# Banded attention unrolled, with its maxima by 32 queries times 160 keys and both score products issued alternately

## The reference, cut to what matters

```
qkv = x @ Wqkv + bqkv;  q, k, v = split(qkv, 3);  16 heads of 8
scores = einsum("bhid,bhjd->bhij", q, k) * 8 ** -0.5
scores = where(|i - j| <= 64, scores, most negative number)
attn = softmax(scores);  out = einsum("bhij,bhjd->bhid", attn, v)
return out @ Wout + bout
```

## Time and profile before

| | |
|---|---|
| median of 3 runs | 861.48 us (861.15 to 864.0) |
| the profiled execution's own time | 861.29 us |
| its span, first to last instruction | 859.5 us |
| attention, first instruction to the next part's first DMA | 0 to 291.88 us |
| busy over the span | PE 77%, DVE 61%, POOL 42%, ACT 40% |
| mean granted TensorE clock | 0.904 of 2.4 GHz |

### The profile page before, as it was taken

One profiled execution on the slowest core, in us unless ns is written; L12 is line 12 of the kernel. 1 busy time (PEld: TensorE's weight loads), 2 busy tenths in 40 slices (PEclk: granted clock), 3 DMA queues, 4 the chain that ended last, 5 costly groups with the idle time before them and its releaser, 6 DMA issues. The chain is left out here.

```text
span 859.5 us, 18332 instructions
## 1 busy us (share of the span) xinstructions
PE 660.1 (77%) x7554; PEld 384.0 (45%) x7554; DVE 525.7 (61%) x1094; ACT 344.9 (40%) x522; POOL 359.2 (42%) x330
## 2 busy tenths in 40 slices
PE   0617888888888279976977498058998988999995
PEld 0302444444445179876876234023333344444442
DVE  8647667676664733342413667869999974406266
ACT  1421433444344573242414552346544536434320
POOL 9202444444444300000001253228999974966530
PEclk9967999999999559997977689669999999999998
DMA  3156552000000364000000640000000000000000
GB/s 76 37 107 108 89 72 32 0 0 0 0 0 2 111 199 100 3 4 2 4 4 5 261 112 0 0 1 0 0 1 0 0 1 1 1 0 1 12 13 25
DMA packets 17327, 29.76 MB, mean 35 GB/s; under 512 B 3248, under 2 KB 13168, under 8 KB 16240
## 3 DMA queue, kind: packets, MB, share of 16 engines
q1 hardware_dynamic: 17264, 28.87, 14.1%
HBM read 24.54 MB, written 4.19 MB: 33 GB/s over the span
## 5 line engine op out<-in xcount | busy, mean ns | idle before, releaser
L474 ACT ACTIVATE pr_exp<-at_psum 128x1024 f32<-128x1024 f32 x68 | 69.6, 1023 | 131.9 <-PE at_psum L559 131.9
L366 DVE TENSOR_REDUCE pr_neg_max<-at_psum 128x4 f32<-128x1024 f32 x68 | 83.2, 1225 | 49.8 <-PE at_psum L541 49.8
L316 POOL TENSOR_SCALAR_AFFINE_SELECT pr_exp<-pr_exp 128x512 f32<-128x512 f32 x68 | 47.1, 692 | 159.0 <-ACT pr_exp L474 159.0
L1493 POOL TENSOR_TENSOR all_phi_b<-all_phi_b,mo_work 128x512 f32<-128x512 f32 x56 | 71.1, 1269 | 43.3 <-ACT mo_work L1699 38.6
L749 POOL TENSOR_TENSOR all_x<-all_x,ff_x_blocks 128x512 f32<-128x512 f32 x3 | 3.8, 1263 | 173.0 <-ACT ff_x_blocks L940 173.0
L1514 PE MATMUL all_psum<-all_phi,mo_xt 128*128 128x512 f32 x128 | 67.1, 651 | 7.3 <-ACT mo_work L1681 5.6
L536 PE MATMUL at_psum<-band_mask,all_ident_bf 128*128 128x512 bf16 x136 | 43.1, 400 | 38.3 <-DVE pr_q_window L359 38.3
L1463 POOL TENSOR_TENSOR mo_work<-mo_work,mo_max 128x1024 f32<-128x1024 f32 x32 | 61.3, 1916 | 22.1 <-DVE mo_max L1755 22.1
L1547 PE MATMUL all_psum<-mo_xt,all_phi_centred 128*128 128x512 f32 x128 | 65.4, 591 | 0.0
L1600 PE MATMUL all_psum<-mo_work,mo_y_slots 128*128 128x512 f32 x128 | 62.5, 595 | 1.8 <-DVE mo_work L1803 1.8
L1699 ACT ACTIVATE mo_work<-all_psum 128x512 f32<-128x512 f32 x64 | 37.7, 601 | 60.6 <-PE all_psum L1547 60.6
(11 more groups left out here) (339 smaller groups left out, 1340.2 us busy)
## 6 DMA issues: line engine op xcount, KB each, us to landing
all_expert_w<-in_expert_w SPq DMA_DIRECT2D x1, 4096.0 KB, 18.3
ff_b_up<-in_b_up SPq DMA_DIRECT2D x1, 2048.0 KB, 10.2
ff_a_up<-in_a_up SPq DMA_DIRECT2D x1, 2048.0 KB, 16.1
ff_w_down<-in_w_down SPq DMA_DIRECT2D x2, 1024.0 KB, 20.5
at_q_stack<-parts_scratch SPq DMA_DIRECT2D x24, 64.0 KB
at_k_stack<-parts_scratch SPq DMA_DIRECT2D x24, 64.0 KB
at_q_stack<-parts_scratch SPq DMA_DIRECT2D x12, 128.0 KB
at_k_stack<-parts_scratch SPq DMA_DIRECT2D x12, 128.0 KB
```

The lines of the kernel that those rows point to most:

```text
L316: nc.gpsimd.affine_select(out=e[:, g, :, 0, :], in_=e[:, g, :, 0, :], compare_op=ALU.is_ge, fill=0.0, base=0, pattern=[[0, GH], [-1, P]], ...
L366: nc.vector.tensor_reduce(negm[:, GH * g:GH * g + GH].rearrange("p (u r) -> p r u", r=2), psum[:, SN + 2 * (g % 2):SN + 2 * (g % 2) + 2, : ...
L474: nc.scalar.activation(e[:, g, :, :, :].rearrange("p h j q -> p (h j q)"), psum[:, ST:ST + 2, :].rearrange("p b n -> p (b n)"), ACT.Exp).t ...
L1493: nc.gpsimd.tensor_tensor(tot[:, ch % 2, :], first, ec[:, ch % 2, j, :], ALU.add).then_inc(added, 1)
```

## The change: what it does

- **Loop.** All 17 windows (`NW`) are written out on every engine, in 8 units of two heads instead of 4 groups of four. The copies of keys, queries and values to fixed places go, with the tiles for them. Before the first step, the naturals of windows 0 and 1 are computed; step s then computes those of window s + 2.
- **Natural product.** Each unit has 8 products of 32 queries and 160 keys (64*32, 49 rows used) in place of four products of 256 keys per four heads. The mask is no longer written by TensorE; VectorE adds it in one `tensor_tensor_reduce` per head that also takes the maximum.
- **Transposed product.** The maxima's three parts are three more rows of the stacks, so the selector products go, and so does their selector. A unit is four products of 52 rows and 128 columns (64*128), with three PSUM banks in rotation for them and three for the naturals.
- **Order on TensorE.** `scores` issues one transposed product, two natural ones, one transposed one and so on; the natural ones belong to the heads of the other row half (`other`).
- **Maxima.** `take_maxima` on ScalarE copies the transposed maxima and issues two DMAs on ScalarE's queue that put them into the query stack.
- **Projections.** x comes in three DMAs. The parts go straight from SBUF to the stacks, high parts first; the HBM scratch is gone. Only the edges of the stacks are filled by GpSimd; six DMAs write the flag row and the rows of ones. The bias of v is folded into a bias row, and the scale into the exponential. W_qkv and its bias are laid out on the host so that the rows come in the right order.
- **Output.** `project` runs one tile at a time inside the loop, and 12 of the 16 tiles are normalised before the last window is done.
- **Warm-up.** 16 products of 512 columns (`keep_warm`) stand before the first naturals and again before step 0.

The diff, cut to its core:

```diff
-    scratch = nc.dram_tensor("parts_scratch", [3, 2, P, T], BF16).ap()
-    kw = b.sb("k_window", [P, 2, NP, 2 * P], BF16)
-    qw = b.sb("q_window", [P, 2, NP, P], BF16)
...
-        with eng.Fori(0, (NS - 3) // 2) as i:
-                nc.vector.tensor_copy(kw[:, wp, :, :], ks[:, :, bass.ds(w * P, 2 * P)])
-                nc.vector.tensor_copy(qw[:, wp, :, :], qs[:, :, bass.ds(w * P, P)]).then_inc(win, 1)
...
+    NW = NT + 1
+    NU = 8
+    QC, WIN = 32, 160
+    FLAG, PARTS = 48, 49
+    WARM = 16
...
+misc_bf = psum[0:3 * H, MISC, 0:64].bitcast(BF16)
+head = lambda m, i: (m % 2, 2 * (m // 2) + i)
+other = lambda m: m ^ 1
...
+def slot_free(pe, n):
+
+    if n < 3:
+        return
+    if n - 3 in proj_at:
+        pe.wait_ge(y_ready, proj_at[n - 3] + 1)
+    else:
+        pe.wait_ge(sn_free, n - 2 - sum(k <= n - 3 for k in proj_at))
...
+        sp.dma_start(x[:, 0:4, :], rows[:, 0:4, :]).then_inc(x_loaded[0], 16)
...
+        for half in range(2):
+            p0 = 64 * half
+            sp.dma_start(ks[p0 + FLAG:p0 + FLAG + 1, :, :], flags[:, :].unsqueeze(1).broadcast_to([1, NP, (NT + 2) * P])).then_inc(rows_in, 16)
+            sp.dma_start(ks[p0 + PARTS:p0 + PARTS + 3, :, :], ones[:, :].unsqueeze(1).broadcast_to([3, NP, (NT + 2) * P])).then_inc(rows_in, 16)
+            sp.dma_start(qs[p0 + FLAG:p0 + FLAG + 1, :, :], ones[0:1, 0:NW * P].unsqueeze(1).broadcast_to([1, NP, NW * P])).then_inc(rows_in, 16)
...
+        def stack(group, kind):
+            r0, r1 = STACKS[group]
+            sp.wait_ge({"h": hi_ready, "m": mid_ready, "l": low_ready}[kind], 2 * r1 // 512)
+            for which, (dst, terms, pad) in enumerate(((qs, TERMS_Q, 64), (ks, TERMS_K, P))):
+                for n, k in enumerate(terms):
+                    if k == kind:
+                        for half in range(2):
+                            p0 = 64 * half + DH * n
+                            sp.dma_start(dst[p0:p0 + DH, :, pad + r0:pad + r1], part[k][64 * half:64 * half + 64, which, r0:r1]).then_inc(stacked[group], 16)
...
+        def split(ch):
+            r0, r1 = CHUNKS[ch]
+            n = r1 - r0
+            for w in range(2):
+                src = psum[:, (2, 4)[w] + ch % 2, 0:n]
+                dve.wait_ge(hi_ready, 2 * ch + w + 1)
+                if ch >= 2:
+                    dve.wait_ge(low_ready, 2 * ch + w - 3)
+                v.scalar_tensor_tensor(out=rest[:, ch % 2, w, 0:n], in0=src, scalar=bqk[:, w:w + 1], in1=part["h"][:, w, r0:r1],
+                                       op0=ALU.add, op1=ALU.subtract).then_inc(rest_ready, 1)
+            for w in range(2):
+                dve.wait_ge(mid_ready, 2 * ch + w + 1)
+                v.tensor_tensor(part["l"][:, w, r0:r1], rest[:, ch % 2, w, 0:n], part["m"][:, w, r0:r1], ALU.subtract).then_inc(low_ready, 1)
...
+        def maxima(w, m):
+            n = nat_unit(w, m)
+            if m == 0 and w >= 1:
+                dve.wait_ge(mt_done, w)
+            dve.wait_ge(sn_done, n + 1)
+            k = NU * w + m
+            if k >= 3:
+                dve.wait_ge(sn_free, k - 2)
+            for i in range(2):
+                r, j = head(other(m), i)
+                last = v.tensor_tensor_reduce(out=masked[:, 2 * (k % 3) + i, :], in0=psum[:, SN + n % 3, WIN * i:WIN * i + WIN], in1=mask[:, :], scale=-1.0, scalar=3.0e38,
+                                              op0=ALU.add, op1=ALU.min, accum_out=nm[:, r, 0, j:j + 1])
+            last.then_inc(sn_free, 1)
...
+        def exps(w, m):
+            n = NU * w + m
+            act.wait_ge(st_done, n + 1)
+            if w >= 1:
+                act.wait_ge(pv_done, NG * (w - 1) + m // 2 + 1)
+            nc.scalar.activation(e[:, m // 2, 2 * (m % 2):2 * (m % 2) + 2, :, :].rearrange("p h j q -> p (h j q)"), psum[:, ST + n % 3, :], ACT.Exp, scale=scale).then_inc(exp_done, 1)
+
+        def take_maxima(w):
+            act.wait_ge(mt_done, w + 1)
+            if w >= 2:
+                act.wait_ge(nm_in[w % 2], 32 * (w // 2))
+            nc.scalar.copy(m_t[:, w % 2, :], misc_bf).then_inc(mt_ready, 1)
+            act.wait_ge(mt_ready, w + 1)
             for half in range(2):
+                p0 = 64 * half + PARTS
+                act.dma_start(qs[p0:p0 + 3, :, w * P:w * P + P], m_t[24 * half:24 * half + 24, w % 2, :]).then_inc(nm_in[w % 2], 16)
...
+        take_maxima(0)
+        take_maxima(1)
+        for s in range(NW):
+            for m in range(NU):
+                exps(s, m)
+                if m == 1 and s >= 1 and s + 1 < NW:
+                    take_maxima(s + 1)
+                if m == 2 and s >= 1:
+                    take_values(s - 1)
+                if m == 2 and s >= 3:
+                    take_y(s - 3)
+                if m == 6 and s >= 1:
+                    take_attn(s - 1)
+            if s == NW - 2:
+                ln_y.root(act, 0, 12, 0)
+        take_values(NW - 1)
+        take_y(NT - 2)
...
+        def keep_warm(n):
+
+            for _ in range(n):
+                nc.tensor.matmul(psum[:, 5, :].rearrange("p (k n) -> p k n", k=4), c["identb"][:, :], c["identb"][:, :].unsqueeze(1).broadcast_to([P, 4, P]), start=True, stop=True)
...
+        def natural(w, m, i, q):
+            n = nat_unit(w, m)
+            r, j = head(other(m), i)
+            rows = slice(64 * r, 64 * r + PARTS)
+            k0 = w * P + q
+            return nc.tensor.matmul(psum[q:q + QC, SN + n % 3, WIN * i:WIN * i + WIN], qs[rows, j, k0:k0 + QC], ks[rows, j, k0:k0 + WIN], start=True, stop=True)
+
+        def open_transposed(w, m):
+            n = NU * w + m
+            if m == 0:
+                pe.wait_ge(nm_in[w % 2], 32 * (w // 2 + 1))
+            if n >= 3:
+                pe.wait_ge(exp_done, n - 2)
+
+        def transposed(w, m, i, b):
+            n = NU * w + m
+            r, j = head(m, i)
+            rows = slice(64 * r, 64 * r + PARTS + 3)
+            return nc.tensor.matmul(psum[:, ST + n % 3, 256 * i + P * b:256 * i + P * b + P], ks[rows, j, (w + b) * P:(w + b) * P + P], qs[rows, j, w * P:w * P + P], start=True, stop=True)
...
+        def scores(s, m):
+
+            open_transposed(s, m)
+            if s + 2 < NW:
+                open_natural(s + 2, m)
+            for i in range(2):
+                for b in range(2):
+                    t = transposed(s, m, i, b)
+                    if s + 2 < NW:
+                        natural(s + 2, m, i, 2 * b * QC)
+                        n = natural(s + 2, m, i, 2 * b * QC + QC)
+            t.then_inc(st_done, 1)
+            if s + 2 < NW:
+                n.then_inc(sn_done, 1)
+
+        def values(w, g):
+            if g == 0 and w >= 1:
+                pe.wait_ge(o_ready, w)
+            pe.wait_ge(sel_done, NG * w + g + 1)
+            for b in range(2):
                 for k in range(GH):
                     h = GH * g + 2 * (k % 2) + k // 2
+                    last = nc.tensor.matmul(psum[32 * k:32 * k + DH + 1, PV, P * g:P * g + P], v9[:, w + b, h, :], e[:, g, k, b, :], start=(b == 0), stop=(b == 1))
+            last.then_inc(pv_done, 1)
...
+        for w in range(2):
+            for m in range(NU):
+                naturals(w, m)
+            maxima_t(w)
+        keep_warm(WARM)
+        for s in range(NW):
+            for m in range(NU):
+                scores(s, m)
+                if m == 0 and s >= 1:
+                    values(s - 1, 2)
+                if m == 1 and s >= 1 and s + 1 < NW:
+                    maxima_t(s + 1)
+                if m == 1 and s >= 3:
+                    project(s - 3)
+                if m == 2 and s >= 1:
+                    values(s - 1, 3)
+                if m == 4 and s >= 1:
                     values_nat(s - 1)
+                if m == 4:
+                    values(s, 0)
+                if m == 6 and s >= 1:
                     attn_t(s - 1)
+                if m == 6:
+                    values(s, 1)
+        values(NW - 1, 2)
+        values(NW - 1, 3)
+        project(NT - 2)
+        values_nat(NW - 1)
+        attn_t(NW - 1)
+        project(NT - 1)
```

More of the change, by code:

```diff
@@ L174, in attention @@
+        bv = a.sb("bv", [P, 1])
         wout = a.sb("wout", [P, P])
[L175 to L205, removed]
[L206 to L569 removed]
@@ new lines, in attention @@
+        bout = a.sb("bout", [1, P])
+        bias = a.sb("bias_row", [1, P])
+        one = a.sb("one_row", [1, P])
+        xn = a.sb("xn", [P, NT, P])
+        y = xn
+        xt = a.sb("xt", [P, T])
+        rest = a.sb("rest", [P, 2, 2, 512])
+        part = {k: a.sb(f"part_{k}", [P, 2, T], BF16) for k in "hml"}
+        ones = a.sb("ones", [3, (NT + 2) * P], BF16)
+        flags = a.sb("flags", [1, (NT + 2) * P], BF16)
+        mask = a.sb("mask", [P, WIN], BF16)
+        masked = a.sb("masked", [P, 6, WIN], BF16)
@@ new lines, in attention @@
+        nm = a.sb("neg_max", [P, 2, 3, NP])
+        m_t = a.sb("neg_max_t", [3 * H, 2, P], BF16)
+        e = a.sb("exp", [P, NG, GH, 2, P])
+        rec = a.sb("rec", [P, H])
```

(30 more changed lines are left out.)

640 lines of the change are left out of this document (296 added, 344 removed).

## The result

The changed kernel takes **976.8 us** (median of 4 runs, 975.5 to 980.2) against 861.3 beside it: ratio 1.134, interval 1.130 to 1.139. It is slower by 115 us. The forecast was 776, faster, and its range ended at 900. Rival 2 (the change of form is paid, at 1.2 GHz) had said 984. Medians and ratios here are of the executions within 1.5% of a kernel's fastest, which leaves out one of six of e11_64x32_fill and three of six of e12_64x32_fill_late_sp, and the latter's profile is of one of those left out (837.3 us).

The account below looks back on a forecast made before the run. PE was taken to bound the loop before, ScalarE after. Front end 57, loop 138.5 and end 11.5 make 207 us, 85 less than before: 861.3 − 85 = 776 us; own range 752 to 812, 8-in-10 range 752 to 900.

Parts of the forecast that it names:

- Rival 2: In `scores`: each change of form is paid, at 1.2 GHz; 984 us, about 930 with half the time there; chance 0.18.
- the lower end: PE in the loop: alternating products in opposite row halves costs nothing; PE needs at most 8.3 us per step.
- the upper end: PE in the loop: 0.10 us paid at each of a unit's 8 changes of form.
- triple 0.51: In `scores` at 1.2 GHz: one transposed and two natural products with their changes of form take 0.51 us.
- what lies beside the triples: PE's other work per step (values, transposes, `project`) at 1.2 GHz: 6.5 us.
- 15 steps 330: Loop at 1.2 GHz: 15 steps, 22.9 us each, with some stretches at the upper clock level, take 330 us.
- steps 15 and 16 with the end 27: Last two steps, without naturals, at 9 and 6.5 us, and the attention's end at 11.5.
- step 0 at 57: Front end: step 0 starts near 57 us instead of 73, bounds 49 and 67.
- rival 3: Loop and front end: ScalarE or VectorE stalls more, steps of 9.8 us; 808 us, still faster; chance 0.08.
- the 0.48: VectorE in the loop: each `tensor_tensor_reduce` takes 0.48 us, the upper bound.
- the front end of 65: Before the loop: the front end lasts 65 us rather than 57.
- the step of 8.2: Loop: ScalarE sets the step at 7.3 us, plus 0.9 of PE's waits; 15 steps take 123 us.

Follow-up runs that it names:

- e11_64x32_fill: e7_all_64x32 with eight idle products of 512 columns (64*32) ahead of each unit; 816.6 us, ratio 0.951.
- e12_64x32_fill_late_sp: e11_64x32_fill with the maxima's DMAs on SyncE's queue and the transposition of the normalised output one unit later; 823.4 us, ratio 0.958.
- e1: The changed kernel with natural products in the same row half as the transposed one they alternate with; 979.2 us, ratio 1.141.
- e4: The changed kernel with eleven patterns of 24 products of 128 columns ahead of step 0; each change cost 0.10 us; its kernel time means nothing.
- e3_one_form: The changed kernel with natural products of the transposed form (128 queries, 256 keys), two per unit; 843.7 us, ratio 0.981.
- e7_all_64x32: The changed kernel with each transposed product cut into four of the natural form, 24 products per unit instead of 12; 834.5 us, ratio 0.972.
- e6_one_form_fill: e3_one_form with two idle products of 512 columns ahead of each unit, one in each row half; 821.5 us, ratio 0.957.
- e10_fill_late: e6_one_form_fill with the transposition of the normalised output and ScalarE's copy of it one unit later; 808.6 us, ratio 0.940.

## Why the prediction was wrong

- **The step that failed** is in the part on PE: "I take the lower end, by L559, which is this very product in these halves". L559's halves stream side by side because all eight of its products have one form. The doubt beside it, that no row showed a change between opposite halves, was the case. Runs e1 and e4 put the value at the upper end: 0.10 us per change, in opposite halves as in one. Of PE's time that is 64 × 0.105 × 15 = 101 us. The Trainium skill's rule (TensorEngine Tiling (Array Packing), section Key Properties: changing the tiling mode, not just the tile, drains the engine) agrees with all of e4's patterns; it had been given less weight than a row that was about something else.
- **The clock** was rival 2's second half and came too. Its 0.18 was too little, and the range was drawn to leave it out. The forecast had the loop at 2.4 GHz. The changes are not the whole reason for the lower level: without any inside a unit, e3_one_form and e7_all_64x32 were granted 0.61 and 0.53.
- **Rival 2's terms** against the trace: triple 0.51, measured 0.46, since the change costs 0.10 to 0.11 at 1.2 GHz, not 0.12; what lies beside the triples 6.5 per step, measured 21.8 − 32 × 0.46 = 7.1; 15 steps 330, measured 317; steps 15 and 16 with the end 27, measured 34.9, at a clock of 0.60. In all 984, measured 976.8.
- **Front end**: step 0 at 57, measured 54.72. The first variance chain is over at 8.3 instead of 7, ScalarE's last projection copy ends at 35.2 instead of 38, and a unit of the first naturals takes 0.49 instead of 0.6. The stack's DMAs take 0.64 us of SyncE each, not 0.47, which the warming products hid.
- **VectorE**: `tensor_tensor_reduce` was put at 0.30, with ends of 0.19 and 0.48. Two lie 0.25 us apart (39.72 and 39.97 in the timeline; the 0.32 of one overlaps the next). L401, from which the 0.30 came, has one operand in PSUM and not two. Of rival 3 its terms fall, the 0.48 and the front end of 65; its kind, PE waiting for VectorE and ScalarE, could not show while PE was the bound, and came up once it was faster (e3_one_form, e6_one_form_fill).
- **ScalarE**: exponential 0.60 as said; two DMA issues 1.49 instead of 0.9. Neither was on the path.
- **The forecast of 776** is short for the kernel without a change of form, too. That one measured 843.7, 821.5 with its clock and 808.6 with one wait less. So the step of 8.2 (ScalarE's 7.3 and 0.9 of waits) was a second term put too low, which the first one hid. In the last kernel's profiled execution (812.2) the attention ends at 242.3 instead of 207, 35 later: step 0 starts at 60.6 instead of 57 (4); from window 2's maxima to window 16's 14 periods take 139.3 us instead of 115 (24), one of them 15.9 with PE waiting for the maxima's DMAs and twelve about 9.6; 7 lie in step 0 and the last two steps. Of the 9.6, 8 × 0.21 = 1.7 are the idle products themselves.

## What to carry to other kernels

A row shows two matmuls streaming side by side only for the forms that it holds: before interleaving two kinds of product, ask whether they take the same rows and columns of the array, and if not, either give them one form (even with more products, or with columns that are thrown away) or issue them in long runs. Cost an interleaved stream by its changes, 0.10 us each for the forms here, then look at the granted clock. And an operation that is moved to another queue waits there for all that was issued before it, in the first steps too, where the queue was fullest here (13 us in e12_64x32_fill_late_sp).

## What the runs showed of the hardware that was not expected

- A change of form costs 0.10 us at 2.4 GHz and 0.10 to 0.11 at 1.2 (the triple of 0.34 and 0.46 us): in these kernels it did not scale with the clock. Products of one form cost nothing on top, in whichever half or strip.
- Work that does nothing made a kernel faster: with 0.21 us of idle products per unit the clock rose from 0.61 to 1.00, and the time fell from 843.7 to 821.5 us.
- PE's busy share did not tell its clock: 312.5 of 312.5 us busy at 0.50 in the changed kernel, 79 of 100 at 1.00 in e6_one_form_fill.
- Two DMAs of maxima had landed only 12 us after their issue while the stacks were being filled (e10_fill_late).
